# Unread matmuls ahead of and between the maxima of the first attention step

## Chip, cores and metric

The kernel runs on one core of a Trainium2 chip. The metric is the device time of one execution in microseconds. Five engines work side by side: PE (TensorE), DVE (VectorE), ACT (ScalarE), POOL (GpSimd) and SP (the queue that issues the DMAs), tied by semaphores only.

## What is computed

Four sequences of 512 positions and 128 features go through a cross attention with 16 heads of 64, a quantised feed-forward, six layers, and a last expert feed-forward. The part around the change is the self attention of the six layers (`HD` is 8, `H` is 16, `B` is 4, `L` is 512):

```python
for i in range(NL):
    xn = _adaln(x, noise_emb, n1_w[i], n1_b[i])
    q, k, v = jnp.split(xn @ qkv_w[i].T, 3, axis=-1)
    q, k = _rope(q.reshape(B, L, H, HD)), _rope(k.reshape(B, L, H, HD))
    scores = jnp.einsum('bqhd,bkhd->bhqk', q, k) / np.float32(np.sqrt(HD))
    w = jax.nn.softmax(scores, axis=-1)
    x = x + jnp.einsum('bhqk,bkhd->bqhd', w, v).reshape(B, L, D) @ so_w[i].T
    ...
```

The softmax subtracts each row's maximum, so the maxima over the keys are computed first, for each head and query.

## The kernel before

The work of the layers is cut into 24 steps, one for each layer and sequence; step 0 is layer 0 of sequence 0. Ahead of them stands the first attention and feed-forward, whose last sequence overlaps step 0. Each engine's program is a list of parts, written out by tables: a part's name with its places in one turn, and a table of guests (`PLACED_TENSOR`) that pulls single parts ahead of others. The order on an engine is thus fixed, and each part starts with the semaphores it waits for.

One step's self attention runs so. PE projects q and k (`qk`, L1681) and v (`v`, L1689). DVE multiplies by cosine and sine (L2135), SP swaps halves (L1244), POOL adds and splits each number into three bf16 parts (L2459 to L2469), and SP copies these parts into stacks of rows (L1288 for q, L1299 for k). PE then makes the scores twice. `maximum` (L1558) computes 64 tiles of 128 queries by 512 keys, each into one of the eight PSUM banks by a list (3, 4, 6, 0, 3, 2, 1, 3, ...), and DVE reduces each tile to its maxima (L2059). After 32 maxima POOL splits their negatives into bf16 parts (`shift`, L2472 to L2478), PE turns them (`shift_turn`, L1566), ACT copies them out (L2305), and one DMA (L1302) sets them into the stack. `scores` (L1546) then computes the shifted scores with keys on the partitions, ACT takes the exponential (L2301), and `weigh` (L1578) multiplies with v. A matmul waits for its bank by `free(b)`: the semaphore of the bank's last reader.

Maxima 0 to 37 of step 0 stand on PE nearly alone; from 38 on they alternate with the scores of step 0. Among the first ones stand guests: `condition` (L1367), matmuls of 128x128 by 128x4 that make the norms' gains, in five pieces. The pieces of 4, 10 and 10 matmuls stand just ahead of `v`, the last, of 10, between maxima 1 and 2. ACT copies each piece out (L2213). SP's `other_rows` (zeros at L1195, then L1199 and L1211) fills the stacks of the other steps; it waits for all of `condition`'s pieces, and stands in SP's queue ahead of the first shift rows:

```python
sp.wait_ge(prep_ps, 1 + len(NORM_PIECES))
zeros(A_K + A_STACK, A_CQ, MASK_SLOT, S)
```

The guest `s_turn` (L1349, transposes for step 1) stands ahead of maximum 36, and `ck` and `cv` (L1704, L1696) come around `shift_turn`.

Of the kernel before, what the change touches and what calls it, by code (L numbers as in the profile page):

```python
# [96 lines left out]
def build(nc, a, out):  # L97

    ctx = ExitStack()
    with ctx:  # L100
        def sb(name, shape, dt=fp32):
            return ctx.enter_context(nc.sbuf_tensor(name, shape, dt))
# [3 lines left out]
        def bank(i):  # L106
            return psum[:, i, :]
# [9 lines left out]
        ident = sb("ident", [P, P])  # L117
# [10 lines left out]
        cosT = sb("cosT", [P, S])  # L128
# [12 lines left out]
        def sem(name):  # L141
            return ctx.enter_context(nc.semaphore(name))
# [158 lines left out]
        def four(t):  # L301
# [3 lines left out]
        in_x0, in_c, in_wv, in_wqk, in_ffn, in_late, in_wl, in_wm, stored = (  # L305
            sem(n) for n in ("in_x0", "in_c", "in_wv", "in_wqk", "in_ffn", "in_late", "in_wl", "in_wm", "stored"))
# [1032 lines left out]
        def tensor_program(handle):  # L1339
            pe = Engine(handle)  # L1340
            owner = {}

            def free(b):
                if b in owner:
                    pe.wait_ge(*owner[b])
# [188 lines left out]
            def out_project(attT, w, b):  # L1534
                for q in range(QT):
                    t = handle.matmul(psum[:, b, q * P:(q + 1) * P], attT[:, q * P:(q + 1) * P], w, start=True, stop=True)  # L1536
                return t

            def part(name, i, m):
                l, bt = divmod(m, B)  # L1540
                if name == "scores":
                    g, k, h = i // 16, i % 16 // GROUP, GROUP * (i // 16) + i % GROUP
                    b, lo = BANKS["scores"][i], ROW * (h % 2)
# [3 lines left out]
                                  start=True, stop=True).then_inc(sc_ps, 1)  # L1547
                    owner[b] = (ex, 64 * m + i + 1)
                if name == "maximum":
                    pair, q, j = i // 8, i % 8 // 2, 1 - i % 2  # L1550
                    b, lo = BANKS["maximum"][i], ROW * j
                    pe.wait_ge(q_rows, 112 * (m + 1))
                    pe.wait_ge(k_rows, 96 * (m + 1))
                    pe.wait_ge(rows, 4 * 16)
                    if m:
                        pe.wait_ge(zeroed, 18 * 16)
                    free(b)
                    handle.matmul(bank(b), q_st[m % 3][lo:lo + ROW, pair, q * P:(q + 1) * P], k_st[bt][lo:lo + ROW, pair, :],  # L1558
                                  start=True, stop=True).then_inc(mx_ps, 1)
                    owner[b] = (mx, 64 * m + i + 1)  # L1560
                if name == "shift_turn":
                    b = BANKS["shift_turn"][i]
# [6 lines left out]
                if name == "weigh":  # L1569
# [3 lines left out]
                    b = BANKS["weigh"][g // 2]  # L1573
                    if g % 2 == 0 and k == 0:
                        free(b)
                    for j in range(GROUP):
                        values = of_head(v[m % 3][:, k, :], GROUP * g + j, g % 2)
                        t = handle.matmul(psum[32 * j:32 * j + (HW if g % 2 else 32), b, :], values, pT[:, i % 2, j, :],  # L1578
                                          start=k == 0, stop=k == QT - 1)
                    t.then_inc(pv_ps, 1)  # L1580
                    owner[b] = (o_sb, HALVES * m + g // 2 + 1)
                if name == "so":
                    b = BANKS["so"][0]
# [4 lines left out]
                if name == "c_turn":  # L1588
                    b = BANKS["c_turn"][0]
# [4 lines left out]
                if name == "cq":  # L1594
                    b = BANKS["cq"][0]
# [4 lines left out]
                if name == "cross_max":  # L1600
# [3 lines left out]
                    b = BANKS["cross_max"][i]  # L1604
# [10 lines left out]
                if name == "cshift_turn":  # L1615
                    b = BANKS["cshift_turn"][0]
# [6 lines left out]
                if name == "cross_scores":  # L1623
                    b, lo = BANKS["cross_scores"][i], ROW * (i % 2)
# [3 lines left out]
                                  start=True, stop=True).then_inc(csc_ps, 1)  # L1628
                    owner[b] = (cex, 16 * m + i + 1)
                if name == "cross_weigh":  # L1630
                    pe.wait_ge(cex, 16 * m + 4 * i + 4)
                    pe.wait_ge(cv_sb, l + 1)
                    b = BANKS["cross_weigh"][i // 2]
                    if i % 2 == 0:
                        free(b)
                    for j in range(GROUP):
                        values = of_head(cv[l % 2][0:C, bt, :], GROUP * i + j, i % 2)
                        t = handle.matmul(psum[32 * j:32 * j + (HW if i % 2 else 32), b, :], values, cpT[0:C, i % 2, j, :],  # L1638
                                          start=True, stop=True)
                    t.then_inc(cpv_ps, 1)  # L1640
                    owner[b] = (co_sb, HALVES * m + i // 2 + 1)
                if name == "co":
                    b = BANKS["co"][0]
# [4 lines left out]
                if name == "f_turn":  # L1648
                    b = BANKS["f_turn"][0]
# [4 lines left out]
                if name == "f1":  # L1654
                    b = BANKS["f1"][i]
# [4 lines left out]
                if name == "f2":  # L1660
                    b = BANKS["f2"][0]
                    pe.wait_ge(ge, 4 * m + 4)
                    free(b)
                    for q in range(QT):
                        for c in range(FC):
                            t = handle.matmul(psum[:, b, q * P:(q + 1) * P], hT[:, c, q * P:(q + 1) * P], wcols(m, W_F2 + c * D, D),  # L1666
                                              start=c == 0, stop=c == FC - 1)
                    t.then_inc(f2_ps, 1)
                    owner[b] = (x_f, m + 1)
                if name == "s_turn":  # L1670
                    b = BANKS["s_turn"][0]
# [4 lines left out]
                if name == "qk":  # L1676
                    b = BANKS["qk"][i]
# [5 lines left out]
                if name == "v":  # L1683
                    b = BANKS["v"][0]
# [7 lines left out]
                if name == "ck" and bt == 0:  # L1692
                    b = BANKS["ck"][0]
# [3 lines left out]
                                  start=True, stop=True).then_inc(ck_ps, 1)  # L1697
                    owner[b] = (ck_ro, 2 * l + 2)
                if name == "cv" and bt == 0:
                    b = BANKS["cv"][0]  # L1700
# [52 lines left out]
            def passes():  # L1753
                for name, i, m in parts(TENSOR, STEPS, PLACED_TENSOR):
                    if m is None:
                        part0(name, i, B - 1)
                    else:
                        part(name, i, m)
# [781 lines left out]
        @block.tensor  # L2540
        def _(eng):
            tensor_program(eng)
# [86 lines left out]
```

## Time and profile before

| | us |
|---|---|
| median of 3 runs (lowest, highest) | 2331.89 (2326.9, 2334.36) |
| the profiled execution | 2330.72 |
| its span | 2328.9 |
| busy: PE, DVE, ACT, POOL | 2174.1, 1996.2, 1701.3, 1088.9 |
| mean granted TensorE clock | 0.97 |

Busy time counts an engine's instructions without register, wait and DMA-issuing ones. A matmul's end is modelled, and PE counts as busy at either clock, so the same work fills twice the time at half the clock. A bracket behind a timeline's row gives the idle time ahead of it and what ended it. In the trace an f32 matmul appears as two records, a bf16 one as one.

### The profile page before, as it was taken

What the parts mean: (1) busy time and instruction counts of PE and PEld (TensorE: products, weight loads), DVE (VectorE), ACT (ScalarE), POOL (GpSimd) and SP (SyncE); (2) the same over time, 40 slices, a digit from 0 to 9 for tenths busy, and PEclk for the clock granted to TensorE, in tenths of its full rate; (3) what the DMA queues carried; (4) which work ended last, traced back from release to release, by engine and by line L of the source; (5) the groups of instructions that cost most, each with busy time, mean ns of one, the idle gap of its engine ahead of it and who ended that gap; (6) DMA issues with size and microseconds to landing.
All of it is one profiled execution on the core that took longest, in us unless ns stands there. A gap on an engine that the chain in (4) does not pass through costs nothing.

```text
span 2328.9 us, 44949 instructions
## 1 busy us (share of the span) xinstructions
PE 2174.1 (93%) x16458; PEld 887.6 (38%) x16458; DVE 1996.2 (86%) x4031; ACT 1701.3 (73%) x3457; POOL 1088.9 (47%) x1348
## 2 busy tenths in 40 slices
PE   6999999999678999999999999999999999999879
PEld 3445455545422233333333333333333333333336
DVE  6778889698789989999999999999999999988435
ACT  4778868688156778787888787787877888777534
POOL 3556657466443344544444444544444445442223
PEclk9999999999679999999999999999999999999869
DMA  2000000000412222212222222222122222221000
GB/s 85 2 1 1 2 1 2 31 1 2 108 47 59 60 78 62 62 49 77 61 74 64 56 76 66 68 62 80 49 62 57 84 63 67 57 60 38 24 21 19
DMA packets 108564, 112.98 MB, mean 49 GB/s; under 512 B 15809, under 2 KB 96951, under 8 KB 107319
## 3 DMA queue, kind: packets, MB, share of 16 engines
q1 hardware_dynamic: 108345, 110.12, 17.1%
q8 instruction: 130, 2.13, 0.4%
q14 instruction: 89, 0.73, 0.1%
HBM read 14.80 MB, written 1.05 MB: 7 GB/s over the span
## 4 chain that ended last, share of the span: by engine, by line
PE 51%; DVE 28%; ACT 9%; issue 4%; POOL 3%; DMA 3%; SPq 2%; DVEq 0%; POOLq 0%; ACTq 0%
DVE A L2059 12%; PE psum L1578 7%; PE psum L1558 5%; PE psum L1546 4%; PE psum L1666 4%; PE psum L1638 4%; PE psum L1479 3%; PE psum L1433 3%; DVE A L2091 3%; ACT A L2301 3%; PE psum L1658 3%; ACT A L2239 3%; DVE A L2135 2%; PE psum L1445 2%; PE psum L1536 2%
## 5 line engine op out<-in xcount | busy, mean ns | idle before, releaser
L2301 ACT ACTIVATE A<-psum 128x512 f32<-128x512 f32 x1536 | 828.1, 599 | 253.6 <-PE psum L1546 237.2
L2059 DVE TENSOR_REDUCE A<-psum 128x1 f32<-128x512 f32 x1536 | 957.9, 679 | 43.2 <-PE psum L1558 41.4
L1558 PE MATMUL psum<-A 64*128 64x512 bf16 x1536 | 448.3, 390 | 30.4 <-issue 12.5
L1546 PE MATMUL psum<-A 64*128 64x512 bf16 x1536 | 422.1, 385 | 23.1 <-ACT A L2301 10.6
L1578 PE MATMUL psum<-A 128*9 128x512 f32 (+1 forms) x3072 | 408.7, 605 | 4.0 <-ACT A L2301 2.0
L2428 POOL TENSOR_TENSOR A<-A,rden 128x512 f32<-128x512 f32 x256 | 266.8, 1068 | 177.4 <-DVE rden L1933 176.7
L2321 ACT ACTIVATE A<-psum 77x512 f32<-77x512 f32 x384 | 219.8, 595 | 45.4 <-PE psum L1627 39.7
L1558 PEld LDWEIGHTS psum<-A 64*128 64x128 bf16 x1536 | 110.4, 94 | 313.8 <-ACT A L2301 88.8
L2447 POOL TENSOR_SCALAR A<-A 128x4 f32<-128x4 f32 x72 | 16.4, 228 | 425.6 <-DVE A L2049 425.3
L1546 PEld LDWEIGHTS psum<-A 64*128 64x128 bf16 x1536 | 101.4, 95 | 290.5 <-ACT A L2301 120.2
L2239 ACT ACTIVATE A<-psum,nm 128x512 f32<-128x512 f32 x256 | 176.2, 688 | 44.9 <-DVE nm L1921 44.0
L2459 POOL TENSOR_TENSOR A<-A 128x512 f32<-128x512 f32 (+1 forms) x78 | 97.0, 1244 | 231.1 <-DMA A<-A 116.1
L2091 DVE TENSOR_REDUCE A<-psum 128x8 f32<-128x616 f32 x192 | 147.9, 793 | 49.9 <-PE psum L1610 49.6
L1917 DVE TENSOR_REDUCE mins<-psum 128x2 f32<-128x1024 f32 x128 | 155.2, 1213 | 5.4 <-PE psum L1433 5.2
L1627 PE MATMUL psum<-A 64*77 64x512 bf16 x384 | 135.0, 417 | 9.8 <-ACT A L2321 5.1
L1433 PE MATMUL psum<-A 64*128 64x512 f32 x512 | 142.0, 618 | 1.8 <-DVE mins L1905 1.8
L2472 POOL CAST A<-A 128x32 bf16<-128x32 f32 (+1 forms) x72 | 15.7, 218 | 205.1 <-DVE A L2059 142.9
L1638 PE MATMUL psum<-A 77*32 77x512 f32 (+1 forms) x768 | 107.3, 638 | 3.3 <-DVE A L2059 3.2
L1445 PEld LDWEIGHTS psum<-ident,A 64*128 64x128 f32 x2048 | 76.0, 139 | 72.9 <-issue 48.8
L1658 PE MATMUL psum<-A,wl 128*128 128x512 f32 x192 | 102.4, 640 | 1.5 <-ACT A L2291 0.9
L1578 PEld LDWEIGHTS psum<-A 128*9 128x9 f32 (+1 forms) x3072 | 54.2, 98 | 122.6 <-issue 88.5
L1939 DVE COPY A<-psum 128x512 f32<-128x512 f32 x128 | 85.3, 684 | 14.9 <-PE psum L1445 14.0
(207 smaller groups left out, 3706.3 us busy)
## 6 DMA issues: line engine op xcount, KB each, us to landing
A<-A SPq DMA_DIRECT2D x456, 128.0 KB, 2.4
A<-A SPq DMA_DIRECT2D x336, 64.0 KB, 2.0
A<-zero SPq DMA_DIRECT2D x51, 128.0 KB, 2.3
wl<-in_wl SPq DMA_DIRECT2D x6, 1024.0 KB, 5.8
A<-A SPq DMA_DIRECT2D x36, 78.0 KB, 2.1
A<-in_nT SPq DMA_DIRECT2D x1, 1664.0 KB, 7.2
A<-in_w SPq DMA_DIRECT2D x2, 512.0 KB, 6.8
A<-in_w SPq DMA_DIRECT2D x1, 1024.0 KB, 6.0
```

The costliest lines, as they stand in the source:

```text
L1433: handle.matmul(bank(b), q_pair[lo:lo + HD0, u % 2, q * P:(q + 1) * P], k_pair[lo:lo + HD0, u % 2, 0:S], start=True, stop=True).then_inc(s ...
L1546: handle.matmul(bank(b), k_st[bt][lo:lo + ROW, h // 2, k * P:(k + 1) * P], q_st[m % 3][lo:lo + ROW, h // 2, :], start=True, stop=True).the ...
L1558: handle.matmul(bank(b), q_st[m % 3][lo:lo + ROW, pair, q * P:(q + 1) * P], k_st[bt][lo:lo + ROW, pair, :], start=True, stop=True).then_in ...
L1578: t = handle.matmul(psum[32 * j:32 * j + (HW if g % 2 else 32), b, :], values, pT[:, i % 2, j, :], start=k == 0, stop=k == QT - 1)
L1638: t = handle.matmul(psum[32 * j:32 * j + (HW if i % 2 else 32), b, :], values, cpT[0:C, i % 2, j, :], start=True, stop=True)
L1658: handle.matmul(bank(b), wcols(m, W_F1 + i * P, P), xnT_f, start=True, stop=True).then_inc(f1_ps, 1)
L2059: handle.tensor_reduce(nm[:, pair // 4, q, j, pair % 4:pair % 4 + 1], bank(BANKS["maximum"][i]), AX.X, ALU.max, negate=True).then_inc(mx, 1)
L2091: handle.tensor_reduce(cnm[:, :, :, i], both, AX.X, ALU.max, negate=True).then_inc(cm, 1)
L2239: handle.activation(p0[r][:, j, :], bank(BANKS0["scores"][i][j]), ACT.Exp, bias=nm0[:, r, j:j + 1], accum_out=c_p[:, n, j, q, C:CP]).then_ ...
L2301: handle.activation(pT[:, block % 2, i % GROUP, :], bank(BANKS["scores"][i]), ACT.Exp, scale=HD1 ** -0.5).then_inc(ex, 1)
L2321: handle.activation(cpT[0:C, g % 2, i % GROUP, :], psum[0:C, BANKS["cross_scores"][i], :], ACT.Exp, scale=HD1 ** -0.5).then_inc(cex, 1)
L2428: handle.tensor_tensor(p0[i % 4][:, j, :], p0[i % 4][:, j, :], rden[:, u % 2, j, q:q + 1].to_broadcast([P, S]), ALU.mult).then_inc(dp, 1)
```

## The change

Ahead of maxima 0, 3, 6 ... 63 of step 0 (22 places) PE runs matmuls that nobody reads: twelve ahead of maximum 0, one at each other place. Each multiplies the 128x128 identity with the 128x512 cosine table, both f32, and writes the bank that the maximum then overwrites. `free(b)` comes before the filler, so a filler waits for the bank's last reader as the maximum did. The wait for `in_late` is for the table's load.

```diff
+            def keep_fed(b, n):
+
+                for _ in range(n):
+                    handle.matmul(bank(b), ident[:, :], cosT[:, :], start=True, stop=True)
+
...
                 if name == "maximum":
                     pair, q, j = i // 8, i % 8 // 2, 1 - i % 2
                     b, lo = BANKS["maximum"][i], ROW * j
+                    if m == 0 and i % 3 == 0:
+                        pe.wait_ge(in_late, 96)
+                        free(b)
+                        keep_fed(b, 1 if i else 12)
                     pe.wait_ge(q_rows, 112 * (m + 1))
                     pe.wait_ge(k_rows, 96 * (m + 1))
                     pe.wait_ge(rows, 4 * 16)
```

PE's list at the beginning of step 0's maxima, before (L1689 is `v`, L1558 a maximum, L1367 `condition`):

```order
L1689 MATMUL psum<-wl,A 128x128 x4
L1558 MATMUL psum<-A 128x512 [waits rows,g_copied,k_rows,q_rows]
L1558 MATMUL psum<-A 128x512
L1367 MATMUL psum<-condT,A 128x4 [waits g_copied]
L1367 MATMUL psum<-condT,A 128x4 x9
L1558 MATMUL psum<-A 128x512 [waits qk_ro]
L1558 MATMUL psum<-A 128x512
```

The same place now (L1698 is `v`, L1542 a filler, L1567 a maximum):

```order
L1698 MATMUL psum<-wl,A 128x128 x4
L1542 MATMUL psum<-cosT,ident 128x512 [waits g_copied]
L1542 MATMUL psum<-cosT,ident 128x512 x11
L1567 MATMUL psum<-A 128x512 [waits rows,k_rows,q_rows]
L1567 MATMUL psum<-A 128x512
L1367 MATMUL psum<-condT,A 128x4 [waits g_copied]
L1367 MATMUL psum<-condT,A 128x4 x9
L1567 MATMUL psum<-A 128x512 [waits qk_ro]
L1542 MATMUL psum<-cosT,ident 128x512
```

Nothing changes places; the wait for bank 3's copy moves to the first filler, and the waits for the rows stay with maximum 0, behind the twelve.

PE's list around the projections of step 1, before (L1546 is a score, L1681 a projection, L1578 `weigh`), from maximum 42 on:

```order
L1558 MATMUL psum<-A 128x512 [waits cv_sb]
L1558 MATMUL psum<-A 128x512
L1558 MATMUL psum<-A 128x512 [waits ex]
L1546 MATMUL psum<-A 128x512 [waits mx]
L1681 MATMUL psum<-A,wl 128x512
L1681 MATMUL psum<-A,wl 128x512 [waits mx]
L1558 MATMUL psum<-A 128x512 [waits ex]
L1558 MATMUL psum<-A 128x512 [waits mx]
L1558 MATMUL psum<-A 128x512 [waits ex]
```

The same place now (L1551 is a score, L1690 a projection):

```order
L1542 MATMUL psum<-cosT,ident 128x512 [waits cv_sb]
L1567 MATMUL psum<-A 128x512 x2
L1567 MATMUL psum<-A 128x512 [waits ex]
L1551 MATMUL psum<-A 128x512 [waits mx]
L1690 MATMUL psum<-A,wl 128x512
L1690 MATMUL psum<-A,wl 128x512 [waits mx]
L1542 MATMUL psum<-cosT,ident 128x512 [waits ex]
L1567 MATMUL psum<-A 128x512
```

A filler now stands ahead of maximum 42 and one ahead of 45, and takes over their waits. No other engine's list changes.

## Rows read from the trace of the kernel before

**Rows 1.** The page's busy time of each engine, over the whole span.

```profile
PE 2174.1 (93%) x16458; PEld 887.6 (38%) x16458; DVE 1996.2 (86%) x4031; ACT 1701.3 (73%) x3457; POOL 1088.9 (47%) x1348
```

**Rows 2.** Busy time by stretch: PE, PEld, DVE, ACT, POOL, then granted clock, DMA share, GB/s.

```profile
598.00:600.00 2.00, 2.00 (x20) 2.00 (x20) 1.93 (x4) 0.09 (x1) 0.00 (x0) 1.00 0.08 16
600.00:602.00 2.00, 2.00 (x12) 2.00 (x13) 1.86 (x13) 0.12 (x1) 0.16 (x1) 0.57 0.25 55
...
658.00:660.00 2.00, 1.43 (x8) 0.27 (x11) 1.52 (x3) 0.00 (x0) 2.00 (x1) 0.92 0.23 57
...
668.00:670.00 2.00, 1.81 (x16) 0.31 (x8) 0.79 (x2) 1.21 (x3) 1.79 (x3) 0.86 0.51 141
...
682.00:684.00 2.00, 1.06 (x5) 0.13 (x3) 2.00 (x4) 1.24 (x3) 1.92 (x3) 0.55 0.00 0
...
688.00:690.00 2.00, 2.00 (x14) 0.65 (x11) 0.76 (x2) 0.80 (x2) 0.00 (x0) 0.74 0.00 0
```

**Rows 3.** Timeline of PE: start, us, engine, line, operation, count, idle before.

```profile
594.87 1.98 PE L1681 MATMUL psum<-A,wl 128*128 128x512 f32 x4 [0.93 <-ACT A L2291]
596.69 6.95 PE L1367 MATMUL psum<-condT,A 128*128 128x4 f32 x48
603.50 2.06 PE L1689 MATMUL psum<-wl,A 128*128 128x128 f32 x8
...
617.40 0.61 PE L1558 MATMUL psum<-A 64*128 64x512 bf16 x2 [11.84 <-issue]
617.94 4.43 PE L1367 MATMUL psum<-condT,A 128*128 128x4 f32 x20
622.30 1.03 PE L1558 MATMUL psum<-A 64*128 64x512 bf16 x3
...
654.99 3.62 PE L1681 MATMUL psum<-A,wl 128*128 128x512 f32 x4
...
666.21 3.06 PE L1578 MATMUL psum<-A 128*32 128x512 f32 x16
...
673.69 1.06 PE L1578 MATMUL psum<-A 128*32 128x512 f32 x8
...
684.07 0.61 PE L1546 MATMUL psum<-A 64*128 64x512 bf16 x2 [0.79 <-ACT A L2301]
```

**Rows 4.** Timeline of DVE, the reductions of the maxima.

```profile
618.01 1.29 DVE L2059 TENSOR_REDUCE A<-psum 128x1 f32<-128x512 f32 x2 [2.74 <-PE psum L1558]
622.94 12.44 DVE L2059 TENSOR_REDUCE A<-psum 128x1 f32<-128x512 f32 x20 [3.64 <-PE psum L1558]
635.55 8.46 DVE L2059 TENSOR_REDUCE A<-psum 128x1 f32<-128x512 f32 x14 [0.17 <-PE psum L1558]
```

**Rows 5.** Busy time by stretch again, three longer stretches of step 0.

```profile
622.90:643.90 21.00, 14.73 (x46) 3.14 (x43) 20.59 (x34) 5.24 (x7) 0.92 (x4) 0.50 0.45 82
643.90:660.00 16.10, 12.28 (x40) 4.44 (x43) 12.03 (x25) 7.90 (x14) 4.35 (x2) 0.55 0.07 18
660.00:680.00 20.00, 13.97 (x85) 3.58 (x78) 18.65 (x40) 8.90 (x16) 11.72 (x16) 0.91 0.36 100
```

**Rows 6.** Timeline of SP, the issuing of its DMAs: start, us of issuing.

```profile
611.69 3.85 SPq L1299 DMA_DIRECT2D A<-A  x6
...
622.39 7.40 SPq L1195 DMA_DIRECT2D A<-zero  x5
...
644.51 1.32 SPq L1239 DMA_DIRECT2D A<-A  x1
645.87 0.91 SPq L1302 DMA_DIRECT2D A<-A  x1
```

**Rows 7.** Timelines of ACT and of POOL.

```profile
599.91 0.20 ACT L2213 ACTIVATE gb<-psum 128x40 f32<-128x40 f32 x1 [2.05 <-PE psum L1367]
...
645.20 0.59 ACT L2305 ACTIVATE A<-psum 64x512 bf16<-64x512 bf16 x1 [3.21 <-PE psum L1566]
...
679.28 0.21 POOL L2472 CAST A<-A 128x32 bf16<-128x32 f32 x1 [6.53 <-DVE A L2059]
```

## Prediction

> **What bounds the kernel now.** I read the page first, then the granted clock by stretch, then the timelines of PE and DVE and the chain of waits around the first step. Over the whole span PE is busy 93% and DVE 86% [rows 1], which says little about this change: all of it lies between 605 us and the last maximum of the first step, reduced just before 679.3 [rows 7]. So the question is which wait ends last there.
>
> The clock is at its upper level (2.4 GHz, granted 1.00) to about 600.3 us and at the lower one (1.2 GHz, 0.50) from there to about 658.3: the means 0.57 over 600 to 602 and 0.92 over 658 to 660 place the two edges [rows 2]. It falls while PE runs the 4-column matmuls of `condition`, before any idle time, and it is low through the 11.84 us in which PE waits for the first step's rows [rows 3]. It rises while PE works without gaps: 3.3 us after the start of the q and k projections at 654.99, 2.3 us after the start of the products at 666.21 (0.86 over 668 to 670 puts the edge at 668.6), and 5.0 us after the start of the dense stretch at 684.07 (edge at 689.0) [rows 2, 3].
>
> What waits in that low stretch? From 622.94 on, DVE reduces maxima back to back: 34 of them in 20.9 us, with 0.17 us of idle time [rows 4], and it is busy 20.59 of the 21.00 us from 622.9 to 643.9, while PE at the low clock is busy only 14.73 [rows 5]. DVE bounds these 21 us, and a faster PE gives nothing there. PE bounds three other places: the second `condition` block, 4.43 us between maxima 1 and 2, for which DVE sits idle 3.64 us [rows 3, 4]; the q and k projections at 654.99 (3.62 us); and the products at 666.21 (3.06 us) [rows 3].
>
> The `condition` block has a second client. SP starts filling the stacks of the other steps only when it is done (622.39), issues them until 645.83, and only at 645.87 issues the row copy that the first scores wait for [rows 6]. ACT gives it those rows' data at 645.79, by the chain over the first 32 maxima [rows 7]. Two chains arrive together, and both begin at the end of `condition`.
>
> **The change part by part.**
>
> *The twelve fillers ahead of maximum 0.* They can start at 605.56, when PE has done v [rows 3]: their bank 3 was copied out by ACT at 600.11 [rows 7]. A filler is an f32 matmul of 128x128 by 128x512, the form of the q and k projections, which the trace writes as two records each. Warm, two of these take 1.82 us from their start (594.87) to the start of the next work (596.69), 0.91 us each; at the low clock 3.62 us, 1.8 each [rows 3]. They begin at the low clock. If it rises r after 605.56, they end at 605.56 + r + (12 - r / 1.8) x 0.91. The three rises above give r between 2.3 and 5, with v's matmuls just ahead it could be 2, and with bad luck 6.3: ends are 617.5, 618.5 (r = 4) and 619.6. Maximum 0 started at 617.40, when its rows landed after SP's last issue (to 615.54) [rows 3, 6]; this is POOL's and SP's work and stays. So the twelve delay it by 0.1 to 2.2 us, 1.1 in the middle.
>
> The Trainium skill (TensorE: Matmul & The Clock Gate, "Back-to-back issue gap") gives a warm matmul about its columns over 2.4 GHz plus 2.5 ns. By that an estimate for twelve is 2.6 us, they would be over at 610 and delay nothing. The trace's f32 form shows over four times that.
>
> *The `condition` block of ten.* It is 20 records. Cold they took 4.43 us; in the warm stretch 598 to 600 exactly 20 took 2.00 [rows 2, 3]. Warm, its end comes at 618.5 + 0.44 (maxima 0 and 1) + 2.0 = 620.9 in place of 622.37: 1.4 us earlier, with bounds of 2.4 (r = 2) and 0.4 (r = 6.3). SP's chain gains the same.
>
> *The twelve single fillers before maxima 3, 6 ... 36.* DVE takes three maxima in some 1.85 us (34 in 20.9). PE took 1.03 for three at the low clock and 0.61 for two, which use different halves of the array's rows and run together [rows 3]; at twice the clock three take about 0.5, with a filler 1.4: they fit. Cold it is 1.03 + 1.8 = 2.8 us, and PE would become the bound. Even warm, some come late, since a filler waits until its bank is read and the maximum only then follows: the one before maximum 3 costs about 0.5 us, that of 12 about 0.4 (maximum 11 has to wait for bank 6), those of 15 and 18 some 0.15. These figures are worked out from which bank each maximum takes and when DVE leaves it; together 1.2 us. DVE starts 1.6 us earlier (the 1.4, and 0.2 since a maximum's own record is shorter at the upper level), so 0.4 is left when maximum 31 is reduced. Behind it the s_turn and filler 36 stand ahead of the shift's transposes: cold s_turn and the transposes took some 0.6 us longer, the filler adds 0.91, so 0.3 goes. The rows for the first scores land 0.1 us earlier, bounds 1.1 earlier to 3 later.
>
> *The nine fillers before maxima 39 to 63.* Here PE alternates scores for ACT, maxima for DVE and products. They add 9 x 0.91 = 8.2 us. A warm clock takes 1.7 us from the projections (3.62 against 1.98), 0.9 from the products (3.06 against 2 x 1.06) [rows 3], and, as an estimate from three cold maxima in 1.03, 0.5 from each three of some 8 scores and maxima ahead of the projections, 1.3: 3.8 us. PE's net is +4.4 us, against 3.8 and 6.0 us of idle time in the two stretches to 660 and 680 [rows 5]. But the filler stands in a fixed place: where PE then waits for something else it is free, where it waited before the filler's place it is paid in full. The one before 48 follows scores that wait for DVE's rotation, and that before 51 a maximum released just then; both are paid; the one before 45 is about covered by the projections' gain. Bounds: all 3.8 gained and all fillers hidden, -3.8; nothing gained and none hidden, +8.2. I take +2.2, half of the net, since idle slots and fixed places speak against each other and no row decides.
>
> After 678 us nothing is added. The clock falls again at about 682.2 [rows 2], when no filler is left to hold it; I count no gain there.
>
> Sum: -0.1 + 2.2 = +2.1 us. The profiled execution took 2330.72 (span 2328.9), 1.17 under the median of three runs, 2331.89. The sum gives 2332.8 on the one and 2334.0 on the other; I say 2333. A measurement of this kernel can tell about 0.3%, 7 us, from no change; this is well inside.
>
> **The rivals.**
>
> *A: the cold time is given back.* For it: 58 us at half clock, with PE busy 5.0 us before 622.4 and 14.73 + 12.28 to 660 (32 in all), and DVE idle 4.1 of the 16.1 us to 660 [rows 3, 5]. If PE were the path for all of it, half of 32 less the late fillers' 8.2 would be some 8 us; 12 if half of them hide: 2319 to 2323, with 2321 as its price. Against it: DVE's 0.4 us of idle time in the 21 to 643.9. Chance 0.10. The Trainium skill (the same page, "Terms") prices throttled time at itself times (1 - K/N): 29 us as its estimate, thus some 2303. The trace bears that out only where PE is the last to arrive, and DVE's rows say it mostly isn't.
>
> *B: the clock falls again in `condition`.* It fell 3.6 us after the start of the first such block [rows 2, 3]; the second is 2.0 us, but PE also waits beside it. Then the first fillers are cold at 1.8 us: DVE idles 1.6 us before maximum 3 and again before 6, and maximum 31 is 2 us later than before. With the late fillers' 2.2, +4 and some more: 2336. Chance 0.13.
>
> *C, slower: the clock doesn't rise, or only late.* Place: the twelve, ahead of maximum 0. At 1.8 us each they end at 627.2, 9.8 us late, and at the low clock each later filler makes three maxima 1.0 us longer (2.8 against 1.85), until the clock is up. That is +10 if it rises with the last of the twelve, +22 if not before maximum 36: 2342 to 2354. Each us of r costs 0.49, so it decides from an r of 14 us. Against it: three rises within 5 us of dense work. This is also the case in which the change doesn't do what it says. Chance 0.08.
>
> *D, slower: the nine late fillers are all on the path.* PE, ACT and DVE wait on each other there in turn, and a 0.91 us filler before each third maximum lengthens the turn: 8.2 - 0.1 = +8.1, 2340. Against it: PE's idle 9.8 us of 36. Chance 0.08.
>
> **How the numbers follow.** The forecast has 0.61. Faster by over 0.3%: rival A and 0.03 of the forecast, 0.13. Slower by over 0.3%: C, D and 0.02 of B, 0.18. Within 0.3%: 0.69. The range runs from A's near end to the near end of C, 2324 (a little above its 2323, since executions of one kernel lie some 3 us either way) to 2341.
>
> **What would show it.** In the new profile: PE's idle 11.84 us gone, twelve f32 matmuls from 605.6, the clock up again 2 to 6 us later, maximum 0 at 617.5 to 619.6, `condition`'s ten at 2.0 us, SP's first zeros at about 621, then 34 reductions in some 22 us with small gaps before 3 and 12, and the first scores at about 648.8. Wrong would be: a second fall right behind `condition`, filler pairs at 1.8 us beyond the fourth, a first score later than 651, or a first step whose last maximum (the one reduced at 679 before) comes more than 4 us earlier or later.

## The result and the profile after

| | before | changed |
|---|---|---|
| median (lowest, highest) of 9 runs each | 2331.44 (2323.62, 2336.26) | 2337.41 (2330.44, 2345.72) |
| the profiled execution, its span | 2330.72, 2328.9 | 2336.08, 2334.3 |
| mean granted clock | 0.970 | 0.981 |

The ratio is 1.0029, with a 95% interval of 1.0015 to 1.0042: 6 us slower by the medians, with a clock that is higher on the whole. The difference is small, but the interval leaves out 1.

Lines of the changed kernel have higher numbers (L1551 is a score, L1567 a maximum, L2068 the reduction, L2481 POOL's shift), and the filler is L1542. In the changed profile the engines are already 0.4 to 0.8 us ahead of before at 603 us, ahead of any filler, so I compare lengths from the start of maximum 0 on PE: to the first score, and to POOL's second shift, which follows the reduction of maximum 63.

The page's busy times and granted clock in 40 slices, against [rows 1]:

```profile
PE 2193.5 (94%) x16517; PEld 893.6 (38%) x16524; DVE 1995.4 (85%) x4031; ACT 1700.0 (73%) x3457; POOL 1088.6 (47%) x1348
...
PEclk9999999999889999999999999999999999999969
```

The two slices that hold 580 to 700 us rose from 6 and 7 to 8 and 8. PE is 19 us busier, the others do what they did. The busy time by stretch (columns as in [rows 2]) tells where the clock moved:

```profile
606.00:608.00 2.00, 2.00 (x4) 0.72 (x3) 1.22 (x2) 0.71 (x3) 1.85 (x3) 0.74 0.56 150
620.00:622.00 2.00, 2.00 (x9) 0.54 (x7) 1.25 (x3) 0.46 (x1) 0.00 (x0) 0.68 0.65 123
626.00:628.00 2.00, 1.72 (x4) 0.10 (x2) 0.97 (x3) 0.00 (x0) 0.00 (x0) 0.62 0.84 147
648.00:652.00 4.00, 1.73 (x13) 1.05 (x11) 3.93 (x7) 1.83 (x3) 0.00 (x0) 0.93 0.05 16
656.00:660.00 4.00, 4.00 (x13) 1.13 (x13) 2.62 (x5) 3.36 (x6) 1.52 (x1) 0.72 0.00 0
```

It rose at about 607.0 (0.74 is half the stretch at each level), 2.3 us after the first filler, fell at 620.7, 1.6 us after the `condition` block, rose at 627.5, fell at 651.4 and rose at 658.2. The timeline of PE, against [rows 3]:

```profile
604.71 11.63 PE L1542 MATMUL psum<-cosT,ident 128*128 128x512 f32 x24
616.49 0.39 PE L1567 MATMUL psum<-A 64*128 64x512 bf16 x2
616.81 2.40 PE L1367 MATMUL psum<-condT,A 128*128 128x4 f32 x20
619.14 0.39 PE L1567 MATMUL psum<-A 64*128 64x512 bf16 x1
...
622.19 2.08 PE L1542 MATMUL psum<-cosT,ident 128*128 128x512 f32 x2 [0.15 <-ACT A L2278]
624.20 1.03 PE L1567 MATMUL psum<-A 64*128 64x512 bf16 x3
...
628.82 1.12 PE L1542 MATMUL psum<-cosT,ident 128*128 128x512 f32 x2
629.88 0.60 PE L1567 MATMUL psum<-A 64*128 64x512 bf16 x3
...
651.00 0.39 PE L1551 MATMUL psum<-A 64*128 64x512 bf16 x1 [0.97 <-DMA A<-A]
...
654.39 2.07 PE L1542 MATMUL psum<-cosT,ident 128*128 128x512 f32 x2
```

The twelve end at 616.3. Maximum 0 starts 1.84 us after the end of SP's last issue for its rows (614.65), as it did before (1.86, [rows 3, 6]): no delay. Condition takes 2.3 us where it took 4.4. A single filler takes 1.06 us warm, from its start to the next work (628.82 to 629.88), and 2.0 cold (622.19 to 624.20). The reductions on DVE, against [rows 4]:

```profile
616.90 1.29 DVE L2068 TENSOR_REDUCE A<-psum 128x1 f32<-128x512 f32 x2 [2.53 <-PE psum L1567]
619.56 0.69 DVE L2068 TENSOR_REDUCE A<-psum 128x1 f32<-128x512 f32 x1 [1.38 <-PE psum L1567]
621.00 1.89 DVE L2068 TENSOR_REDUCE A<-psum 128x1 f32<-128x512 f32 x3 [0.75 <-PE psum L1567]
624.85 1.89 DVE L2068 TENSOR_REDUCE A<-psum 128x1 f32<-128x512 f32 x3 [1.96 <-PE psum L1567]
627.76 1.89 DVE L2068 TENSOR_REDUCE A<-psum 128x1 f32<-128x512 f32 x3 [1.02 <-PE psum L1567]
630.30 1.89 DVE L2068 TENSOR_REDUCE A<-psum 128x1 f32<-128x512 f32 x3 [0.66 <-PE psum L1567]
632.53 1.89 DVE L2068 TENSOR_REDUCE A<-psum 128x1 f32<-128x512 f32 x3 [0.34 <-PE psum L1567]
634.76 2.71 DVE L2068 TENSOR_REDUCE A<-psum 128x1 f32<-128x512 f32 x4 [0.34 <-PE psum L1567]
638.27 8.88 DVE L2068 TENSOR_REDUCE A<-psum 128x1 f32<-128x512 f32 x14 [0.80 <-PE psum L1567]
```

The 3.64 us of idle time behind condition are down to 1.38. In their place, gaps stand before maxima 3, 6, 9, 12, 15, 18 and 22, each but the last right at a filler. The 0.75 us before maximum 3 still fall to the upper clock: its filler took 1.06 us (619.45 to 620.51) and the clock fell only at 620.7. The 2.98 us before 6 and 9 stand behind the two fillers that ran at the low clock, and the 2.14 in the last four fall to the upper clock again. The one before 22 comes from a bank that ACT still reads. SP and POOL, against [rows 6, 7]:

```profile
619.24 7.48 SPq L1195 DMA_DIRECT2D A<-zero  x5
...
641.39 1.32 SPq L1239 DMA_DIRECT2D A<-A  x1
648.90 0.61 SPq L1302 DMA_DIRECT2D A<-A  x1
```

```profile
685.79 0.21 POOL L2481 CAST A<-A 128x32 bf16<-128x32 f32 x1 [9.58 <-DVE A L2068]
```

SP's chain is done at 642.7 and now waits 6 us for the shift: of the two chains that arrived together, the one over the maxima alone is late. From maximum 0 to the first score it is 34.51 us (31.56 before), to the second shift 69.30 (61.88 before). Those 7.4 us, less the 0.9 that this execution was ahead and 1.2 that it made good behind 686, are the 5.4 by which the two profiled executions differ.

### The profile page after: what moved, and what is told of

Its sections match the earlier page's. It is cut to its first block, busy times and chain, and to the rows that moved or that the text cites. A ratio compares the mean times of both kernels' runs of the same rounds, so it can differ in the third digit from the quotient of the medians.

```text
span 2334.3 us, 45073 instructions
## 1 busy us (share of the span) xinstructions
PE 2193.5 (94%) x16517; PEld 893.6 (38%) x16524; DVE 1995.4 (85%) x4031; ACT 1700.0 (73%) x3457; POOL 1088.6 (47%) x1348
## 4 chain that ended last, share of the span: by engine, by line
PE 53%; DVE 27%; ACT 10%; issue 3%; POOL 3%; DMA 2%; SPq 1%; another core or an unknown queue 0%; DVEq 0%; POOLq 0%; ACTq 0%
DVE A L2068 13%; PE psum L1587 8%; PE psum L1567 5%; PE psum L1551 5%; PE psum L1675 4%; PE psum L1479 3%; PE psum L1667 3%; PE psum L1647 3%; DVE A L2100 3%; ACT A L2248 3%; PE psum L1433 3%; ACT A L2310 2%; DVE A L2144 2%; PE psum L1636 2%; PE psum L1536 2%
## 5 line engine op out<-in xcount | busy, mean ns | idle before, releaser
L2068 DVE TENSOR_REDUCE A<-psum 128x1 f32<-128x512 f32 x1536 | 957.3, 676 | 51.8 <-PE psum L1567 49.7
L1567 PE MATMUL psum<-A 64*128 64x512 bf16 x1536 | 443.9, 386 | 11.5 <-DVE A L2068 4.5
L1551 PE MATMUL psum<-A 64*128 64x512 bf16 x1536 | 422.4, 385 | 22.6 <-ACT A L2310 10.5
L1567 PEld LDWEIGHTS psum<-A 64*128 64x128 bf16 x1536 | 110.0, 94 | 301.0 <-ACT A L2310 84.8
L1551 PEld LDWEIGHTS psum<-A 64*128 64x128 bf16 x1536 | 101.3, 95 | 289.8 <-ACT A L2310 121.4
L2468 POOL TENSOR_TENSOR A<-A 128x512 f32<-128x512 f32 (+1 forms) x78 | 96.6, 1238 | 230.2 <-DMA A<-A 124.1
L2481 POOL CAST A<-A 128x32 bf16<-128x32 f32 (+1 forms) x72 | 15.7, 218 | 214.0 <-DVE A L2068 150.5
```

Source lines behind the costliest of these rows:

```text
L1551: handle.matmul(bank(b), k_st[bt][lo:lo + ROW, h // 2, k * P:(k + 1) * P], q_st[m % 3][lo:lo + ROW, h // 2, :], start=True, stop=True).the ...
L2068: handle.tensor_reduce(nm[:, pair // 4, q, j, pair % 4:pair % 4 + 1], bank(BANKS["maximum"][i]), AX.X, ALU.max, negate=True).then_inc(mx, 1)
```

## Experiments

Each was also profiled; a length is that of its one profile.

| kernel | ratio [95%] | to first score | on to second shift | sum |
|---|---|---|---|---|
| before | 1 | 31.56 | 30.32 | 61.88 |
| before, once more | (one run) | 31.59 | 30.67 | 62.26 |
| changed | 1.0029 [1.0015, 1.0042] | 34.51 | 34.79 | 69.30 |
| the twelve alone | 1.0001 [0.9992, 1.0010] | 29.28 | 31.96 | 61.24 |
| twelve + early singles | 1.0003 [0.9992, 1.0014] | 34.50 | 30.32 | 64.82 |
| late singles alone | 1.0019 [1.0007, 1.0031] | 31.59 | 35.16 | 66.75 |
| all singles, no twelve | 1.0033 [1.0020, 1.0046] | 37.56 | 34.15 | 71.71 |
| condition moved, no filler | 0.9983 [0.9970, 0.9996] | 26.78 | 30.88 | 57.66 |
| quarter singles | 1.0012 [1.0003, 1.0022] | 32.81 | 33.26 | 66.07 |
| late singles doubled | 1.0054 [1.0038, 1.0069] | 31.57 | 42.73 | 74.30 |
| condition moved, seven, early singles | 1.0005 [0.9992, 1.0018] | 29.51 | 29.26 | 58.77 |
| condition moved, seven | 0.9980 [0.9964, 0.9997] | 26.58 | 30.95 | 57.53 |

The row of the kernel before, profiled twice, says how far a length can be trusted: 0.03 us in the first part, some 0.4 in the second.

**The change taken apart.** Four kernels, each the changed one with another choice of places:

```diff
-                    if m == 0 and i % 3 == 0:
+                    if m == 0 and i == 0:
```

> Only the twelve fillers ahead of maximum 0; no single ones. Lengths are taken in the trace from the start of maximum 0: to the first score 31.56 us in the kernel before, 34.51 in the changed one; to POOL's second shift 61.88 and 69.30. Theory 1 (each single filler costs where it stands, the twelve are free): condition's ten take 2.0 to 2.4 us in place of 4.43, the first score comes after 29.2 to 29.6 us, the second shift after 59.5 to 60, and the time is about 2.3 us under the kernel before, 2329. Theory 2 (the single fillers only cost because the clock fell again under them): the same here. A rival: the clock falls behind condition as it did in the changed kernel (at 620.7) and stays low without the singles; then the length from maximum 2 to the first score is as before, since DVE bounds it, and the time is the same 2329. Wrong for both: a second shift after more than 62 us.

The first score came after 29.28 us, as theory 1 had it, and the clock fell at 622.2 without harm: DVE went through 34 maxima as before, 12.43 and 8.46 us long against 12.44 and 8.46 in [rows 4].

```profile
622.68 12.43 DVE L2068 TENSOR_REDUCE A<-psum 128x1 f32<-128x512 f32 x20 [1.55 <-PE psum L1567]
635.28 8.46 DVE L2068 TENSOR_REDUCE A<-psum 128x1 f32<-128x512 f32 x14 [0.18 <-PE psum L1567]
```

But only 0.6 of the 2.3 us were left at the second shift (61.24, where 59.5 to 60 was expected), and none in the time: the expected 2.3 us under before is a miss. A part may have gone to the clock: from the first score to the second shift its mean was 0.72 here, against 0.79 and 0.78 in the two profiles of before. No run isolates this.

```diff
-                    if m == 0 and i % 3 == 0:
+                    if m == 0 and i % 3 == 0 and i < 38:
```

> The twelve and the twelve single fillers before maxima 3 to 36; none from 39 on. Theory 1: the first score as in the changed kernel, after 34 to 34.6 us; from there to the second shift as before (30.3 us) or up to 1 less where the clock is up, so the second shift after 64 to 65 us, and the time 2.5 to 3 us above before: 2334. Theory 2 (only the low clock makes the singles dear): the cost depends on whether the clock falls behind condition; with the clock up throughout, the first score would come after 29.5 to 30.5 us and the time would be 2329 to 2330.

The first part is the changed kernel's to 0.01 us, the second the one of before. So the early singles cost 34.50 - 29.28 = 5.2 us at the first score, which turns the twelve's gain of 2.3 into a loss of 2.9. The clock fell behind `condition` here too, at about 622.6, so this run can't tell the cost of the place from that of the clock. The time, +0.7 us by the ratio with an upper end of 3.3, is under what was expected.

```diff
-                    if m == 0 and i % 3 == 0:
+                    if m == 0 and i % 3 == 0 and i > 38:
                         pe.wait_ge(in_late, 96)
                         free(b)
-                        keep_fed(b, 1 if i else 12)
+                        keep_fed(b, 1)
```

> Only the nine single fillers before maxima 39 to 63; neither the twelve nor the early ones. Theory 1: the first score as before, after 31.4 to 31.7 us; from there to the second shift 34.8 us as in the changed kernel against 30.3 before, so the second shift after 66 to 67 us, and the time +4.5 us: 2336. Theory 2: the fillers start at the low clock here and the first ones cost 1.8 us each until it rises, so the second part is at least as long as in the changed kernel, 35 to 37 us.

The late singles alone cost 35.16 - 30.32 = 4.8 us, and the time rises by 4.4. That is what theory 1 expected, but 35.16 lies in theory 2's range as well, so this run doesn't part the two. The stretches from the first score to the second shift, before, here, and in the changed kernel, say where the 4.8 us come from (columns as in [rows 2], the length first):

```profile
648.96:679.28 30.32, 22.48 (x103) 5.70 (x103) 24.97 (x56) 15.41 (x28) 15.50 (x15) 0.79 0.25 70
```

```profile
648.98:684.14 35.16, 29.30 (x118) 7.92 (x118) 25.34 (x55) 15.07 (x27) 15.51 (x15) 0.89 0.22 60
```

```profile
651.00:685.79 34.79, 28.93 (x118) 7.91 (x118) 26.42 (x56) 15.06 (x27) 15.51 (x14) 0.90 0.22 61
```

From their starts to the next work the nine fillers hold PE for 10.95 us here: the first two, in part at the low clock, for 2.01 and 1.63, the others for 0.95 to 1.06. Yet PE is only 6.82 us busier. By this difference its other work took 4.1 us less at the higher clock; 1.6 of it is seen at the projections (1.98 against 3.62 in [rows 3]) and 1.1 at the products (1.92 against 3.06). PE's idle time, the length less the busy time, shrank from 7.84 to 5.86 us, by 2.0. So 10.95 - 4.1 - 2.0 = 4.8. In the changed kernel the same terms are 10.82, 4.4 and 2.0, and 4.5 are left.

```diff
-                    if m == 0 and i % 3 == 0:
+                    if m == 0 and i % 3 == 0 and i > 0:
...
-                        keep_fed(b, 1 if i else 12)
+                        keep_fed(b, 1)
```

> All 21 single fillers, without the twelve. Theory 1: condition's ten are cold (4.43 us), the singles start cold and make PE the bound until the clock rises, then cost what they did: the first score after 36.5 to 38 us, the second shift after 71 to 73 us, the time +9 to +11 us over before: 2341. Rival (the twelve are what costs, the singles hide behind DVE once the clock is up): the first score after less than 33 us and the time within 3 us of before.

All singles without the twelve: 37.56 and 71.71 us, both as theory 1 had them, and 1.0033, 7.7 us, a little under the +9. With the changed kernel at 1.0029, the twelve are worth next to nothing in time, though 3.05 us at the first score. The three parts add up: -2.3 + 5.2 + 4.8 = +7.7 us against the measured 7.4. Taken at the second shift alone, the first two are smaller, and their sum is the same: the twelve give 0.6 and the early singles cost 64.82 - 61.24 = 3.6.

**What a single filler costs.** Doubled:

```diff
-                    if m == 0 and i % 3 == 0:
+                    if m == 0 and i % 3 == 0 and i > 38:
...
-                        keep_fed(b, 1 if i else 12)
+                        keep_fed(b, 2)
```

> Two fillers instead of one before each of maxima 39 to 63, and none elsewhere. One each made the way from the first score to the second shift 35.2 us in place of 30.3. Theory 1 (each is paid in full or to some fixed part): a second one has no idle time left to hide in and costs its full 0.91 us warm, up to 1.8 for the first while the clock is low: 35.2 + 8 to 10 = 43 to 45 us, the second shift after 75 to 77 us, the time +12 to +14: 2344. Theory 2 (idle slots still hide most): under 40 us for that way and a time of at most 2339.

```profile
657.09 1.98 PE L1542 MATMUL psum<-cosT,ident 128*128 128x512 f32 x4
659.01 0.60 PE L1567 MATMUL psum<-A 64*128 64x512 bf16 x3
```

A pair takes 1.92 us (657.09 to 659.01), the second thus 0.86. Nine of these are 7.7 us, and the way to the second shift grew by 42.73 - 35.16 = 7.6. The second filler is paid in full.

```profile
649.24:691.97 42.73, 36.69 (x136) 11.41 (x136) 25.48 (x55) 15.18 (x27) 15.54 (x15) 0.91 0.18 50
```

PE's idle time is 6.04 us here, against 5.86 with one filler at each place: the second one found nothing to hide in. Nor does it earn clock time, since the mean was 0.89 already and is 0.91. The nine first ones cost 4.8 us, about half of 9 x 1.06, but by the rows above this is mostly time that the higher clock gave back, and only 2.0 us of idle time filled. Theory 1 is right on the second filler (its 43 to 45 a little high, its time of 2344 against 2342.86).

Cut to a quarter of the columns, the twelve left whole:

```diff
                 for _ in range(n):
-                    handle.matmul(bank(b), ident[:, :], cosT[:, :], start=True, stop=True)
+                    w = S if n > 1 else P
+                    handle.matmul(psum[:, b, 0:w], ident[:, :], cosT[:, 0:w], start=True, stop=True)
```

> The changed kernel with its 21 single fillers cut to a quarter (128 of 512 columns, 0.23 us warm); the twelve stay whole. Theory 1 (a single filler costs by its length, behind its bank's wait): the losses at the singles shrink to about a quarter, the first score comes after 29.5 to 31 us and the second shift after 61 to 63.5, the time is within 2 us of before. Theory 2 (what costs is that a filler stands between the bank's release and the maximum at all, or that it breaks up pairs of maxima): the first score after 33 us or more, the time +4 or more. The clock will tell by the way whether quarter fillers hold it.

Both theories missed: 32.81 lies between them, and so does the time, some 2.8 us over before; 66.07 lies above theory 1's range. What neither had is the clock:

```profile
620.00:624.00 4.00, 3.73 (x18) 1.73 (x16) 3.49 (x6) 0.60 (x1) 0.00 (x0) 0.61 0.71 131
624.00:628.00 4.00, 2.80 (x8) 0.80 (x6) 3.33 (x7) 0.00 (x0) 0.00 (x0) 0.50 0.84 150
640.00:644.00 4.00, 3.58 (x11) 1.33 (x10) 3.32 (x7) 2.55 (x3) 0.92 (x4) 0.50 0.12 25
656.00:660.00 4.00, 4.00 (x13) 1.56 (x9) 2.85 (x5) 2.09 (x4) 2.80 (x1) 0.70 0.00 0
```

It fell at about 620.9 and stayed down to 658.4, where in the changed kernel, with whole fillers at the same places, it was up again at 627.5. And at the low clock a quarter filler held PE for 0.73 us:

```profile
621.48 0.80 PE L1543 MATMUL psum<-cosT,ident 128*128 128x128 f32 x2 [0.27 <-ACT A L2279]
622.21 1.03 PE L1568 MATMUL psum<-A 64*128 64x512 bf16 x3
```

That is 0.69 of a whole one's 1.06 at the upper level, and the twelve early ones cost 32.81 - 29.28 = 3.5 us, 0.68 of 5.2. So this run fits a price by the time that a filler holds PE. As two of the twelve whole ones were cold, at 2.0 us, and nearly all of the quarter ones, the agreement is partly luck.

**Why the clock fell, and what it cost.** Condition's last piece stood between maxima 1 and 2. Here it goes into PE's idle time ahead of maximum 0, first with no filler anywhere:

```diff
-                        ("maximum", 2, 0): [("condition", 3, None)],
+                        ("maximum", 0, 0): [("condition", 3, None)],
```

> No fillers at all: the kernel before with its last piece of condition (ten matmuls) moved from between maxima 1 and 2 to ahead of maximum 0, into PE's idle time. Theory 1 (DVE bounds the maxima, and what the twelve fillers gained they gained through condition alone): condition runs cold from 605.6 to about 610, DVE reduces from maximum 0 on without the 3.6 us of idle time, the first score comes after 27.5 to 28 us from maximum 0 (31.56 before). Of this 3.5 to 4 us the run with the twelve fillers alone lets one expect that a part is lost again before the second shift (it had 2.28 at the first score and 0.64 there): the second shift after 58.5 to 61 us, the time 1 to 4 us under before. Rival (the clock matters by itself, so that without fillers nothing is gained): the second shift after 61.5 to 62.5 us.

```profile
605.58 4.27 PE L1367 MATMUL psum<-condT,A 128*128 128x4 f32 x20
618.93 1.03 PE L1558 MATMUL psum<-A 64*128 64x512 bf16 x4 [9.08 <-issue]
```

```profile
619.55 13.63 DVE L2059 TENSOR_REDUCE A<-psum 128x1 f32<-128x512 f32 x22 [4.03 <-PE psum L1558]
633.36 8.46 DVE L2059 TENSOR_REDUCE A<-psum 128x1 f32<-128x512 f32 x14 [0.18 <-PE psum L1558]
```

Condition is done, cold, by 609.9. DVE reduces 36 maxima with 0.18 us of idle time between the first and the last, and the first score comes 4.8 us earlier than before, the second shift 4.2, both more than expected. SP's chain starts earlier too, with its zeros at 617.78 in place of 622.39: both chains that began behind `condition` gain. The median is 2324.67 against 2329.44 of before on the same chip, a ratio of 0.9983 [0.9970, 0.9996]: some 4 us faster than before, by an interval that just leaves out 1, with no unread matmul. (The profiled execution itself took 2333.76, and that of the last kernel below 2322.04 with the same lengths to 0.2 us: executions also differ by some 10 us in what lies behind the first step.)

The same with seven fillers behind condition, and the early singles:

```diff
-                        ("maximum", 2, 0): [("condition", 3, None)],
+                        ("maximum", 0, 0): [("condition", 3, None)],
...
-                    if m == 0 and i % 3 == 0:
+                    if m == 0 and i % 3 == 0 and i < 38:
...
-                        keep_fed(b, 1 if i else 12)
+                        keep_fed(b, 1 if i else 7)
```

> Condition's last piece moved ahead of maximum 0, seven fillers behind it in what is left of the idle time, and the twelve single fillers before maxima 3 to 36; none from 39 on. In the changed kernel the clock fell just after condition, and DVE lost 3.7 us before maxima 3, 6 and 9, then 2.1 at 12 to 22 with the clock up. Theory 1 (condition between the maxima made the clock fall, and about 3 of the early singles' 5.2 us come from the low clock, 2 from their place): the clock is up from about 612 to past 645, the first score comes after 28.8 to 29.8 us (26.8 with condition moved and no fillers). Theory 2 (the fall has nothing to do with condition: maxima at DVE's pace don't hold the clock even with fillers): it falls within 10 us of maximum 0, and the first score comes after 30.5 us or more.

```profile
612.00:616.00 4.00, 4.00 (x9) 1.73 (x8) 2.46 (x5) 0.00 (x0) 3.84 (x5) 0.75 0.71 202
624.00:628.00 4.00, 2.66 (x8) 0.80 (x8) 3.34 (x7) 0.00 (x0) 0.00 (x0) 1.00 0.44 84
640.00:644.00 4.00, 3.14 (x13) 1.11 (x13) 4.00 (x7) 1.13 (x1) 0.92 (x4) 1.00 0.02 6
648.00:652.00 4.00, 3.33 (x12) 0.69 (x12) 2.80 (x11) 2.81 (x6) 0.93 (x1) 0.51 0.00 0
```

```profile
618.18 3.68 DVE L2068 TENSOR_REDUCE A<-psum 128x1 f32<-128x512 f32 x6 [3.65 <-PE psum L1567]
622.23 3.68 DVE L2068 TENSOR_REDUCE A<-psum 128x1 f32<-128x512 f32 x6 [0.38 <-PE psum L1567]
626.57 1.89 DVE L2068 TENSOR_REDUCE A<-psum 128x1 f32<-128x512 f32 x3 [0.66 <-PE psum L1567]
```

The clock is up from 614 to 648: with condition out of the way and the same singles in place it didn't fall, so theory 1 has the fall right. DVE's gap before maximum 3 is gone and the one before 6 is 0.38 us; those before 12, 15, 18 and 22 are the 2.14 us of the changed kernel, unchanged. The first score comes after 29.51 us, 2.7 later than with no fillers. That is what the early singles cost by their place, at a clock that is up. Of the changed kernel's 5.2 us the other 2.5 came with condition between the maxima. The low clock's part of them is at most 1.8, by subtraction, for 0.75 stands before maximum 3, at a filler that ran at the upper level: DVE had run dry behind condition, and had no tile left to reduce while the filler ran. The second shift comes 3.1 us earlier than before, but the time doesn't show it (1.0005, at best 1.9 us under before). That is the widest gap between a length and a time in the table, and it stays open.

With the move, the seven and no single filler (the move's lines as above):

```diff
-                    if m == 0 and i % 3 == 0:
+                    if m == 0 and i == 0:
...
-                        keep_fed(b, 1 if i else 12)
+                        keep_fed(b, 7)
```

> Condition's last piece moved ahead of maximum 0 and seven fillers behind it, no single ones. Theory 1 (with condition out of the way a warm clock ahead of the maxima has nothing left to shorten, since DVE bounds them): the first score after 26.5 to 27 us, as with condition moved and no fillers (26.78), the second shift after 57 to 59, the time that of that run, 2325. Rival (fillers help by themselves): the first score after less than 26 us and a time lower by over 2 us.

26.58 and 57.53 us, against 26.78 and 57.66 with no fillers, and a ratio of 0.9980 [0.9964, 0.9997] against 0.9983. The clock was up from 613.5 to 623.7; it made no difference.

```profile
622.00:624.00 2.00, 0.34 (x3) 0.00 (x0) 2.00 (x5) 0.00 (x0) 0.00 (x0) 0.93 0.85 145
```

So condition isn't needed for a fall: here the clock fell long behind the last matmul of 4 columns (609.3), 6.1 us into maxima that waited for DVE, with PE busy for 0.34 of the 2.00 us around the fall. What the twelve had gained, they had gained through condition alone.

**The start of maximum 0.** It lay at 619.4 with the twelve alone, 2 us behind the last filler, and the kernel before was profiled a second time for this.

> The kernel before, unchanged, once more. Maximum 0 started at 617.4 in its profile, in those with fillers from 616.5 to 619.4, and at 618.9 with condition moved and no fillers. If the place of maximum 0 scatters from execution to execution by the landing of the row DMAs, this one may lie anywhere from 616.5 to 619.5 with the first score 31.6 us behind it; if the later starts came from the changes, it lies at 617.4.

It lay at 618.15, 0.75 later than in the first profile, with the first score 31.59 us behind it. So the start moves without any change to the kernel. Here all of it came from further ahead: SP's first issue of the swap (L1244) stood at 600.99 in place of 600.20. The time from that issue to POOL's first part behind it (L2459 or L2468) was 4.1 us in nine of the twelve profiles and 5.7, 5.3 and 5.1 in three, one of them the run with condition moved and no filler at all. Others with the twelve fillers, and others with condition moved, are among the nine at 4.1. So a landing that varies, and no edit, fits the three latest starts.

## Why the prediction was right, point by point

The time, 2337.41, lies in the range, and the sign was right, but the forecast's 2333 was 4 us low. By its steps:

- *The twelve fillers ahead of maximum 0*: the clock rose 2.3 us behind their start, near the early bound of 2, and they took 11.6 us where the early end has 11.9. They delayed nothing; 1.1 us was forecast.
- *The `condition` block of ten*: 1.4 us earlier was forecast, 2.5 of shortening less the delay of 1.1; 2.3 was measured from maximum 0 (29.28 against 31.56), within the bounds of 0.4 to 2.4.
- *The twelve single fillers before maxima 3, 6 ... 36* is the first step that failed. It had the clock up throughout; instead the fall of rival B came true, 1.6 us behind condition. B's places were off by one: the filler before maximum 3 still ran at the upper level, and the cold ones stand before 6 and 9. Its "DVE idles 1.6 us before maximum 3 and again before 6" is 0.75, 1.96 and 1.02 before 3, 6 and 9. The first score came 2.95 us late where the sum had 0.1 early. At a clock that is up the singles cost 2.7 us, in place of the step's 1.5 (1.2, and 0.3 behind maximum 31): a single filler holds PE for 1.06 us and not the 0.91 of one in a row of two, the gaps before 12, 15 and 18 are about twice what was worked out, and the one before 22 was not seen. The other 2.5 us, of which at most 1.8 are the low clock's, had no term in the sum.
- *The nine fillers before maxima 39 to 63*: the mechanism was right and the size off, 4.5 us in the changed kernel where the step had 2.2. The clock gave back 4.4 us (forecast 3.8), and idle time hid 2.0, about the 2.2 that "half of the net" left hidden. The term that was mis-sized is the fillers' own "9 x 0.91 = 8.2": they held PE for 10.8 us, since a single one takes 1.06 and the first two, in part at the low clock, took 2.0 and 1.5. That the halving came out is luck, for it was a choice between two bounds.
- *Rival A* fell: mean clock up by a hundredth, time up by 6 us. The Trainium skill's rule (TensorE: Matmul & The Clock Gate, "Terms") prices throttled time at itself times (1 - K/N), whatever PE's work waits for. The traces disagree where PE isn't the last to arrive: some 10 us of raised clock ahead of and under maxima that wait for DVE were worth 0.2 us (26.78 against 26.58).
- *Rival C* fell with the rise at 607.0. *Rival D* priced all nine late fillers as on the path at +8.1 us; 4.5 were paid.

The sum with measured sizes is -2.3 + 5.2 + 4.5 = +7.4 us at the second shift. What became of the 1.2 us made good behind it was not followed. That the time stayed in the range owes something to the range's width: the sum to the second shift was short by 5.3 us.

## What to carry to other kernels

In this step a low clock cost time only where its engine arrived last. Before filling idle time to raise the clock, look for the work that the idle time could hold. Here the ten small matmuls that the fillers made faster could be put into the gap itself: 4.8 us at the first score, with nothing added. And a filler in a stream that another engine paces isn't free even where the engine's busy time leaves room: it stands between a bank's release and the work that waits for it. Of the 10.8 us that the nine late ones held PE, idle time hid 2.0, and of a second one at each place nothing.

## What the runs showed of the hardware

- The clock fell during or just behind matmuls of 4 columns with PE busy without a gap, at 600.3 in the kernel before and at 620.7 in the changed one. With the small matmuls moved away and the same singles in place it stayed up for 34 us. With them moved away and no singles it fell as well, 6.1 us into maxima that waited for DVE.
- With one f32 filler of 512 columns before each third maximum the clock came up again at 627.5; with one of 128 columns it stayed low to 658.4. At the low level a short filler held PE for 0.73 us, with a quarter of the columns; a whole one at the upper level held it for 1.06.
- A landing of one group of DMAs, in nine profiles at 4.1 us from the first issue, took 5.1, 5.3 and 5.7 in three others, which starts the first maximum up to 1.6 us later. The repeat of the kernel before started it 0.75 us later with a landing at 4.1.
